# GpSimd in a state-space scan: the row product of a pair moves from the first place to the second

## The chip, the core and the metric

The kernel is written for one core of one Trainium2 chip, each engine's instructions by hand, with semaphores between them. A core has TensorE (PE, the matrix unit, with its weight loads as PEld), VectorE (DVE), ScalarE (ACT), GpSimd (POOL) and SyncE (SP, which issues DMAs here). An engine works through its own queue in order. The metric is the device time of a run in microseconds; the number to predict is the median of such runs.

## What is computed

Two layers follow each other over x of shape 4 x 1024 x 128: attention with a mixture of experts, and then a selective state-space layer (Mamba) with a second mixture of experts. The change lies in the recurrence of the state-space layer:

```python
dA = jnp.exp(dt_t[..., None] * A)
hstate = dA * hstate + (dt_t * u_t)[..., None] * B_t[:, None, :]
y_t = jnp.einsum('bdn,bn->bd', hstate, C_t)
...
y = jnp.swapaxes(ys, 0, 1) + u * D
y = y * jax.nn.silu(z)
```

There are 256 channels and 16 states to a channel; `A` depends on channel and state, `B_t` and `C_t` are one number for each state and time step, shared by all channels.

## The kernel before

`mamba_scan` keeps 128 channels on the 128 partitions, so the 256 channels make two halves (`half` 0 and 1), and time (1024 steps) runs along the free dimension. For each of 4 sequences it goes through the 16 states, two at a time: that is a pair `p`, 8 to a sequence (`JB`), 32 in all. Within a pair, `odd` 0 and 1 is the first and the second state. One tile of work is always 128 x 1024 numbers. For a pair the engines do this (written with (odd, half)):

- PE, **spread** (L1685, two matmuls in bf16): writes the row B of a state to all partitions of a PSUM tile, for (0,0), (0,1) and (1,0). There are two such PSUM tiles, one for each half (`inputs(half)`), so a spread waits until the last scan that read the tile is done.
- DVE, **input** (L1746): multiplies the spread row by `dtu`, which is dt * u (L1741, `times_u`, once for a sequence and half), in PSUM. Three of them in a pair.
- POOL, **row product** (L1808, `ms_x_row`): the same product for the fourth combination (1,1), from `b_row` in SBUF, a row of B brought in by a DMA.
- ACT: the decays exp(dt * A) (L1729 for three scans, L1732 for the fourth, into PSUM).
- DVE, **scan** (L1759): the recurrence, four in a pair, (0,0), (0,1), (1,0), (1,1), each into its own part of `h` (the tile `xnT` in the profile).
- POOL, **weigh** (L1801, `ms_ch`): the scanned state times the row C, four in a pair, into one of two tiles, one for each half. It waits for the scan of the same (odd, half), for the row of C, and for the add that read the tile before.
- PE, **add** (L1694, four matmuls in f32 against the identity, `x4` in the profile): adds the weighed state into the sums of its half in PSUM.
- In pairs 4 and 5 of a sequence PE adds u * D too (L1701, `skip`); at the first pair of the next sequence DVE reads the sums out (L1764, `gate`), between its scans.
- SP: loads `b_row` for a pair when the row product of the pair before is done (L1671), and after it the two rows of C (L1665) into a ring of four.

All loops are unrolled, and what stands in them sets the order of each queue. DVE, in a pair: input (0,0), input (0,1), scan (0,0), scan (0,1), input (1,0), scan (1,0), scan (1,1). At the end of a sequence `times_u` for the next stands behind scan (1,0) and behind scan (1,1). PE:

```python
for p in range(PAIRS_ALL):
    spread(p, 1, 0)
    add(p, 0, 0)
    if p + 1 < PAIRS_ALL:
        spread(p + 1, 0, 0)
    add(p, 0, 1)
    if p + 1 < PAIRS_ALL:
        spread(p + 1, 0, 1)
    add(p, 1, 0)
    ...
    add(p, 1, 1)
```

POOL, in a pair: row product, weigh (0,0), weigh (0,1), weigh (1,0), weigh (1,1). The row product waits for its row of B, for `dtu`, and for scan (1,1) of the pair before, which reads `x_row`; scan (1,1) of its own pair waits for it.

Of the kernel before, what the change touches and what calls it, by code (L numbers as in the profile page):

```python
# [1360 lines left out]
DI = 2  # L1361
# [256 lines left out]
def mamba_scan(nc, g, m):  # L1618


    with ExitStack() as ctx:
# [29 lines left out]
        def scans(p, odd, half):  # L1651

            return 4 * p + 2 * odd + half + 1
# [5 lines left out]
        @block.sync  # L1659
        def _(sp):  # L1660
            def c_row(p, odd):
                s = 2 * p + odd
                if p >= C_RING // 2:
                    sp.wait_ge(ch_ready, scans(p - C_RING // 2, odd, 1))
                sp.dma_start(c_rows[:, s % C_RING, :], g.bc_rows[NS + s % NS:NS + s % NS + 1, sequence(s // NS)].to_broadcast([P, T])).then_inc(c_in[s % C_RING], 16)  # L1665

            for p in range(PAIRS_ALL):
                n, b = 2 * p % NS + 1, p // JB
                if p > 0:
                    sp.wait_ge(x_row_ready, p)  # L1670
                sp.dma_start(b_row[:, :], g.bc_rows[n:n + 1, sequence(b)].to_broadcast([P, T])).then_inc(b_in, 16)  # L1671
                c_row(p, 0)
                c_row(p, 1)
# [115 lines left out]
        @block.gpsimd  # L1789
        def _(pool):  # L1790
            for half in range(DI):
                pool.tensor_tensor(diag[:, half, :], g.ident[:, :], m.d[:, half:half + 1].to_broadcast([P, P]), ALU.mult).then_inc(diag_ready, 1)

            def weigh(p, odd, half):
                s = 2 * p + odd
                if half == 0:
                    pool.wait_ge(c_in[s % C_RING], C_BASE + 16 * (s // C_RING + 1))
                pool.wait_ge(scanned, scans(p, odd, half))
                if s > 0:
                    pool.wait_ge(summed, scans((s - 1) // 2, (s - 1) % 2, half))  # L1800
                pool.tensor_tensor(ch[:, half, :], h[:, odd, half, :], c_rows[:, s % C_RING, :], ALU.mult).then_inc(ch_ready, 1)  # L1801

            for p in range(PAIRS_ALL):
                pool.wait_ge(b_in, 16 * (p + 1))
                pool.wait_ge(dtu_ready, DI * (p // JB) + 2)
                if p > 0:
                    pool.wait_ge(scanned, scans(p - 1, 1, 1))
                pool.tensor_tensor(x_row[:, :], dtu[:, 1, :], b_row[:, :], ALU.mult).then_inc(x_row_ready, 1)  # L1808
                for odd in range(2):
                    for half in range(DI):  # L1810
                        weigh(p, odd, half)


def mamba_out(nc, g, m):
# [352 lines left out]
```

## Time and profile before

| | us |
|---|---|
| three timed runs | 1480.87, 1481.11, 1486.27 |
| median | 1481.11 |
| the profiled execution: its own time | 1482.99 |
| its span, first to last instruction | 1481.1 |
| `mamba_scan` in it, from the first `times_u` to the last `gate` | 881.9 to 1307.4, 425.5 |

| engine | busy in the whole span, us | busy from 898 to 1300 us, of 402 us |
|---|---|---|
| PE | 1214.6 | 310.85 |
| DVE | 1153.7 | 391.20 |
| ACT | 672.6 | 132.41 |
| POOL | 653.5 | 364.15 |

In the profile a line names the source line, the engine, the operation, what is written and read, the shapes and how many instructions are merged. `[2.19 <-POOL ms_ch L1801]` behind it says that the engine was idle 2.19 us before and that POOL's product on L1801 ended this. The times are starts, counted from the start of the span, and durations. On DVE and POOL a duration overlaps the next instruction's start by 0.05 to 0.1 us, so a chain on one engine is measured from start to start; ends on PE are modelled. The granted clock (PEclk) is 1.00 at 2.4 GHz and 0.50 at 1.2 GHz.

### The profile page before, as it was taken

How to read it: one execution, taken by the hardware profiler on the slowest of the kernel's cores; microseconds unless marked ns; L12 is line 12 of the kernel's file. 1: busy time of each engine (PE TensorE's matmuls, PEld its weight loads, DVE VectorE, ACT ScalarE, POOL GpSimd, SP SyncE). 2: the span in 40 equal slices, each digit the busy share in tenths (PEclk: the TensorE clock that was granted, in tenths of full speed). 3: DMA queues.
4: the chain of work that ended last, by engine and by line, in shares of the span. 5: the costliest groups of instructions: out<-in, count | busy, mean ns of one | idle time of the engine just before them, and what ended most of it. 6: DMA issues, size and time to landing. Idle time of an engine off the chain costs nothing. (4 is left out here: it accounts for less than half of the span.)

```text
span 1481.1 us, 21354 instructions
## 1 busy us (share of the span) xinstructions
PE 1214.6 (82%) x7478; PEld 548.8 (37%) x7478; DVE 1153.7 (78%) x1366; ACT 672.6 (45%) x1057; POOL 653.5 (44%) x468
## 2 busy tenths in 40 slices
PE   4937999998999789879978767877877867766998
PEld 2412334333344344444444212322322322355565
DVE  5868999998996256747556889999999999964554
ACT  2515999997897413212215783333333323302221
POOL 2320000101002166636743068989989989921000
PEclk9956999999999889989997868999999999995999
DMA  4321111312101443313520013343333333400331
GB/s 105 121 94 44 57 50 51 115 48 77 50 25 46 103 112 112 110 57 105 120 50 18 6 51 128 128 128 104 117 119 128 128 100 115 126 9 24 68 57 43
DMA packets 75346, 120.37 MB, mean 81 GB/s; under 512 B 13246, under 2 KB 42758, under 8 KB 75254
## 3 DMA queue, kind: packets, MB, share of 16 engines
q1 hardware_dynamic: 75254, 119.16, 27.2%
q8 instruction: 56, 0.92, 0.3%
q14 instruction: 36, 0.29, 0.1%
HBM read 105.09 MB, written 13.63 MB: 80 GB/s over the span
## 5 line engine op out<-in xcount | busy, mean ns | idle before, releaser
L635 DVE TENSOR_REDUCE att_found<-PS 128x2 f32<-128x1024 f32 (+2 forms) x288 | 333.2, 1219 | 17.9 <-PE PS L738 16.1
L705 ACT ACTIVATE att_prob<-PS 128x512 f32<-128x512 f32 x576 | 313.6, 596 | 42.5 <-PE PS L760 30.5
L1694 PE MATMUL PS<-ms_ch,ident_sb 128*128 128x512 f32 x512 | 269.0, 651 | 72.6 <-POOL ms_ch L1801 72.6
L1801 POOL TENSOR_TENSOR ms_ch<-xnT,ms_c_rows 128x1024 f32<-128x1024 f32 x128 | 304.8, 2392 | 41.3 <-DVE xnT L1759 21.3
L1759 DVE TENSOR_TENSOR_SCAN xnT<-ms_decay,PS 128x1024 f32<-128x1024 f32 x96 | 216.1, 2276 | 4.2
L779 PE MATMUL PS<-att_prob,att_v 128*32 128x256 f32 (+1 forms) x2560 | 183.9, 374 | 2.8 <-ACT att_out L694 2.6
L1694 PEld LDWEIGHTS PS<-ms_ch,ident_sb 128*128 128x128 f32 x512 | 98.6, 204 | 194.8 <-POOL ms_ch L1801 107.5
L1732 ACT ACTIVATE PS<-m_dt,m_a 128x1024 f32<-128x1024 f32 x32 | 35.8, 1118 | 260.5 <-DVE xnT L1759 260.5
L738 PE MATMUL PS<-kr,qr 55*128 55x128 bf16 (+4 forms) x1152 | 121.4, 292 | 30.8 <-PEq L260 15.6
L760 PE MATMUL PS<-qr,kr 55*128 55x128 bf16 (+4 forms) x1152 | 115.3, 278 | 15.5 <-ACT att_prob L705 9.1
L1746 DVE TENSOR_TENSOR PS<-ms_dtu,PS 128x1024 f32<-128x1024 f32 x96 | 114.7, 1213 | 6.8 <-PE PS L1685 6.7
L1183 ACT ACTIVATE f_h<-PS,e_w_b 128x512 f32<-128x512 f32 x64 | 44.0, 687 | 159.3 <-PE PS L1311 159.3
L1729 ACT ACTIVATE ms_decay<-m_dt,m_a 128x1024 f32<-128x1024 f32 x96 | 106.2, 1138 | 13.3 <-DVE xnT L1759 13.3
L1162 POOL TENSOR_TENSOR f_yT<-f_yT,f_prod 128x512 f32<-128x512 f32 x56 | 70.9, 1267 | 93.6 <-DVE f_prod L1260 92.3
L1250 DVE SCALAR_TENSOR_TENSOR f_x3s<-PS,e_w_b,f_mask_row 128x512 f32<-128x512 f32 x64 | 47.9, 749 | 75.3 <-PE PS L1315 73.7
L1151 POOL TENSOR_TENSOR f_xm<-xnT,f_gate_row 128x512 f32<-128x512 f32 x64 | 81.0, 1267 | 40.1 <-DMA f_gate_row<-gate_rows_dram 37.9
L1685 PE MATMUL PS<-m_bc,m_w_sel_b 96*128 96x512 bf16 x192 | 64.0, 419 | 33.8 <-DVE xnT L1759 25.2
L738 PEld LDWEIGHTS PS<-kr,qr 48*128 48x128 bf16 (+1 forms) x1152 | 39.7, 97 | 137.7 <-issue 89.5
L779 PEld LDWEIGHTS PS<-att_prob,att_v 128*32 128x32 f32 x2560 | 55.1, 109 | 63.0 <-issue 53.7
L1808 POOL TENSOR_TENSOR ms_x_row<-ms_dtu,ms_b_row 128x1024 f32<-128x1024 f32 x32 | 75.2, 2348 | 1.7 <-DMA ms_b_row<-bc_rows_dram 1.7
L1320 PE MATMUL PS<-f_h,e_w_w 128*128 128x512 f32 x128 | 66.9, 605 | 10.8 <-DVE f_prod L1260 10.8
L1759 DVE TENSOR_TENSOR_SCAN xnT<-PS,ms_x_row 128x1024 f32<-128x1024 f32 x32 | 72.5, 2266 | 0.0
(222 smaller groups left out, 1632.5 us busy)
## 6 DMA issues: line engine op xcount, KB each, us to landing
ms_c_rows<-bc_rows_dram SPq DMA_DIRECT2D x64, 512.0 KB, 5.9
f_gate_row<-gate_rows_dram SPq DMA_DIRECT2D x64, 256.0 KB, 3.4
ms_b_row<-bc_rows_dram SPq DMA_DIRECT2D x32, 512.0 KB, 3.6
f_mask_row<-mask_rows_dram SPq DMA_DIRECT2D x64, 128.0 KB, 3.0
qk_parts_dram<-qkv_parts SPq DMA_DIRECT2D x48, 128.0 KB, 1.9
heads_dram<-att_out SPq DMA_DIRECT2D x16, 256.0 KB, 2.7
f_mask_row<-mask_rows_dram SPq DMA_DIRECT2D x64, 64.0 KB, 3.3
qr<-qk_parts_dram SPq DMA_DIRECT2D x32, 96.0 KB
```

Of the source, the lines that this page charges most:

```text
L635: dve.tensor_reduce(found[:, :, pair, first:first + (n - 1) * step + 1:step], PS[:, bank:bank + 2, :].rearrange("p r (w n) -> p r w n", w= ...
L705: act.activation(prob[:, step % PROB_RING * GH + h, :], PS[:, SCORE_BANK + unit % SCORE_RING, :], ACT.Exp, scale=float(D) ** -0.5).then_in ...
L738: last = pe.matmul(PS[:, MAX_BANK + 2 * (m % 2) + r, at:at + n], rows(qr, count, i, pair, r, q_block * P, P), rows(kr, count, i, pair, r, ...
L760: last[r] = pe.matmul(PS[:, SCORE_BANK + (unit + r) % SCORE_RING, col:col + w], rows(kr, count, i, pair, r, j * P, P), rows(qr, count, i, ...
L779: last = pe.matmul(PS[VW * h:VW * (h + 1), VALUE_BANK, q - half * CH:q - half * CH + w], v1[:, i % 2, half, h, j, :], prob[:, step % PROB_ ...
L1151: pool.tensor_tensor(xm[:, e % XM_RING, :], xnT[:, c * CH:(c + 1) * CH], gate_row[:, e % ROW_RING, :], ALU.mult).then_inc(xm_ready, 1)
L1694: last = pe.matmul(PS[:, Y_BANK + 2 * half + q, :], g.ident[:, :], ch[:, half, q * CH:(q + 1) * CH], start=j == 0 and not odd, stop=j == J ...
L1729: act.activation(decay[:, 2 * odd + half, :], m.dt[:, half, sequence(b)], ACT.Exp, scale=m.a[:, half, n + odd:n + odd + 1]).then_inc(decay ...
L1746: dve.tensor_tensor(inputs(half), dtu[:, half, :], inputs(half), ALU.mult).then_inc(input_ready, 1)
L1759: dve.tensor_tensor_scan(h[:, odd, half, :], factor, x, 0.0, ALU.mult, ALU.add).then_inc(scanned, 1)
L1801: pool.tensor_tensor(ch[:, half, :], h[:, odd, half, :], c_rows[:, s % C_RING, :], ALU.mult).then_inc(ch_ready, 1)
L1808: pool.tensor_tensor(x_row[:, :], dtu[:, 1, :], b_row[:, :], ALU.mult).then_inc(x_row_ready, 1)
```

## The change

In POOL's part of `mamba_scan` the first weigh of a pair is put ahead of the row product. Nothing else is touched: the same instructions with the same waits, 5 to a pair on POOL, in the order weigh (0,0), row product, weigh (0,1), weigh (1,0), weigh (1,1).

```diff
@@ -1801,14 +1801,15 @@
             for p in range(PAIRS_ALL):
+                weigh(p, 0, 0)
                 pool.wait_ge(b_in, 16 * (p + 1))
                 pool.wait_ge(dtu_ready, DI * (p // JB) + 2)
                 if p > 0:
                     pool.wait_ge(scanned, scans(p - 1, 1, 1))
                 pool.tensor_tensor(x_row[:, :], dtu[:, 1, :], b_row[:, :], ALU.mult).then_inc(x_row_ready, 1)
-                for odd in range(2):
-                    for half in range(DI):
-                        weigh(p, odd, half)
+                weigh(p, 0, 1)
+                weigh(p, 1, 0)
+                weigh(p, 1, 1)
```

POOL's queue for pairs 2 and 3, with the semaphores that each instruction waits for. `ms_ch` is a weigh, `ms_x_row` the row product, `ring_in0` to `ring_in3` the landing of a row of C (0 and 1 for the two states of an even pair, 2 and 3 for those of an odd one). Before:

```order
L1808 TENSOR_TENSOR ms_x_row<-ms_dtu,ms_b_row 128x1024 [waits ms_scanned,ms_dtu_ready,ms_b_in]
L1801 TENSOR_TENSOR ms_ch<-xnT,ms_c_rows 128x1024 [waits ms_summed,ms_scanned,ring_in0]
L1801 TENSOR_TENSOR ms_ch<-xnT,ms_c_rows 128x1024 [waits ms_summed,ms_scanned]
L1801 TENSOR_TENSOR ms_ch<-xnT,ms_c_rows 128x1024 [waits ms_summed,ms_scanned,ring_in1]
L1801 TENSOR_TENSOR ms_ch<-xnT,ms_c_rows 128x1024 [waits ms_summed,ms_scanned]
L1808 TENSOR_TENSOR ms_x_row<-ms_dtu,ms_b_row 128x1024 [waits ms_scanned,ms_dtu_ready,ms_b_in]
L1801 TENSOR_TENSOR ms_ch<-xnT,ms_c_rows 128x1024 [waits ms_summed,ms_scanned,ring_in2]
```

The same place of POOL's queue in the changed kernel (the row product's line is now L1809):

```order
L1801 TENSOR_TENSOR ms_ch<-xnT,ms_c_rows 128x1024 [waits ms_summed,ms_scanned,ring_in0]
L1809 TENSOR_TENSOR ms_x_row<-ms_dtu,ms_b_row 128x1024 [waits ms_scanned,ms_dtu_ready,ms_b_in]
L1801 TENSOR_TENSOR ms_ch<-xnT,ms_c_rows 128x1024 [waits ms_summed,ms_scanned]
L1801 TENSOR_TENSOR ms_ch<-xnT,ms_c_rows 128x1024 [waits ms_summed,ms_scanned,ring_in1]
L1801 TENSOR_TENSOR ms_ch<-xnT,ms_c_rows 128x1024 [waits ms_summed,ms_scanned]
L1801 TENSOR_TENSOR ms_ch<-xnT,ms_c_rows 128x1024 [waits ms_summed,ms_scanned,ring_in2]
```

The row product has changed places with weigh (0,0): the row product of a pair now stands behind an instruction that waits for a scan of that pair, and so does the load of the next rows, which SP issues behind it. Everything from weigh (0,1) on stands where it stood.

POOL's queue at the last pair, before:

```order
L1808 TENSOR_TENSOR ms_x_row<-ms_dtu,ms_b_row 128x1024 [waits ms_scanned,ms_dtu_ready,ms_b_in]
L1801 TENSOR_TENSOR ms_ch<-xnT,ms_c_rows 128x1024 [waits ms_summed,ms_scanned,ring_in2]
L1801 TENSOR_TENSOR ms_ch<-xnT,ms_c_rows 128x1024 [waits ms_summed,ms_scanned]
L1801 TENSOR_TENSOR ms_ch<-xnT,ms_c_rows 128x1024 [waits ms_summed,ms_scanned,ring_in3]
L1801 TENSOR_TENSOR ms_ch<-xnT,ms_c_rows 128x1024 [waits ms_summed,ms_scanned]
L1621 UNCONDITIONAL_BRANCH
```

and after:

```order
L1801 TENSOR_TENSOR ms_ch<-xnT,ms_c_rows 128x1024 [waits ms_summed,ms_scanned,ring_in2]
L1809 TENSOR_TENSOR ms_x_row<-ms_dtu,ms_b_row 128x1024 [waits ms_scanned,ms_dtu_ready,ms_b_in]
L1801 TENSOR_TENSOR ms_ch<-xnT,ms_c_rows 128x1024 [waits ms_summed,ms_scanned]
L1801 TENSOR_TENSOR ms_ch<-xnT,ms_c_rows 128x1024 [waits ms_summed,ms_scanned,ring_in3]
L1801 TENSOR_TENSOR ms_ch<-xnT,ms_c_rows 128x1024 [waits ms_summed,ms_scanned]
L1621 UNCONDITIONAL_BRANCH
```

Here too four weighs and one row product stand before the end of the stage, and the row product comes second.

## Rows read from the trace of the kernel before

**Rows 1.** Windows: stretch, us; busy PE, PEld, DVE, ACT, POOL; clock, DMA
```profile
898.00:1300.00 402.00, 310.85 (x712) 115.72 (x711) 391.20 (x229) 132.41 (x121) 364.15 (x156) 0.94 0.36 118
```

**Rows 2.** Waits of DVE from 885 to 1308 us: total, times, longest
```profile
DVE PS L1746 <- PE PS L1685: 6.7, 12, 1.3
DVE m_u L1764 <- PE PS L1694: 3.4, 2, 2.4
```

**Rows 3.** Timeline of one pair at the full clock: start, duration, what
```profile
1005.20 4.46 DVE L1759 TENSOR_TENSOR_SCAN xnT<-ms_decay,PS 128x1024 f32<-128x1024 f32 x2
1005.70 2.36 POOL L1808 TENSOR_TENSOR ms_x_row<-ms_dtu,ms_b_row 128x1024 f32<-128x1024 f32 x1
1005.80 1.99 PE L1694 MATMUL PS<-ms_ch,ident_sb 128*128 128x512 f32 x4 [0.38 <-POOL ms_ch L1801]
1007.62 0.60 PE L1685 MATMUL PS<-m_bc,m_w_sel_b 96*128 96x512 bf16 x2
1008.00 4.68 POOL L1801 TENSOR_TENSOR ms_ch<-xnT,ms_c_rows 128x1024 f32<-128x1024 f32 x2
...
1010.91 2.29 DVE L1759 TENSOR_TENSOR_SCAN xnT<-ms_decay,PS 128x1024 f32<-128x1024 f32 x1
1013.11 2.27 DVE L1759 TENSOR_TENSOR_SCAN xnT<-PS,ms_x_row 128x1024 f32<-128x1024 f32 x1
1013.25 0.61 PE L1685 MATMUL PS<-m_bc,m_w_sel_b 96*128 96x512 bf16 x2 [0.86 <-DVE xnT L1759]
1013.33 4.75 POOL L1801 TENSOR_TENSOR ms_ch<-xnT,ms_c_rows 128x1024 f32<-128x1024 f32 x2 [0.65 <-DVE xnT L1759]
...
1015.29 2.33 DVE L1746 TENSOR_TENSOR PS<-ms_dtu,PS 128x1024 f32<-128x1024 f32 x2
...
1017.54 2.28 DVE L1759 TENSOR_TENSOR_SCAN xnT<-ms_decay,PS 128x1024 f32<-128x1024 f32 x1
```

**Rows 4.** Timeline of the next pair, where the add runs slowly
```profile
1022.74 3.64 PE L1694 MATMUL PS<-ms_ch,ident_sb 128*128 128x512 f32 x4 [2.19 <-POOL ms_ch L1801]
...
1028.37 0.60 PE L1685 MATMUL PS<-m_bc,m_w_sel_b 96*128 96x512 bf16 x2
...
1029.07 1.23 DVE L1746 TENSOR_TENSOR PS<-ms_dtu,PS 128x1024 f32<-128x1024 f32 x1 [0.23 <-PE PS L1685]
```

**Rows 5.** Windows, columns as in Rows 1: the stretch of the slow add
```profile
1022.70:1026.10 3.40, 3.36 (x4) 1.28 (x5) 3.27 (x3) 3.08 (x4) 2.30 (x1) 0.50 0.98 325
```

**Rows 6.** The weigh's line: duration ns min/median/max, first and last start
```profile
L1801 POOL TENSOR_TENSOR ms_ch<-xnT,ms_c_rows x128: 2335/2356/3252, 889.5 to 1301.7; 128x1024 f32<-128x1024 f32 x128
```

**Rows 7.** Timeline at the end of the second sequence: times_u beside weighs
```profile
1089.10 1.20 DVE L1741 TENSOR_TENSOR ms_dtu<-m_dt,m_u 128x1024 f32<-128x1024 f32 x1
...
1089.31 6.51 POOL L1801 TENSOR_TENSOR ms_ch<-xnT,ms_c_rows 128x1024 f32<-128x1024 f32 x2 [0.66 <-DVE xnT L1759]
...
1092.41 1.20 DVE L1741 TENSOR_TENSOR ms_dtu<-m_dt,m_u 128x1024 f32<-128x1024 f32 x1
```

**Rows 8.** Timeline in the first mixture of experts: both engines read two SBUF tiles
```profile
586.60 1.26 POOL L1162 TENSOR_TENSOR f_yT<-f_yT,f_prod 128x512 f32<-128x512 f32 x1 [7.10 <-DVE f_prod L1260]
586.62 1.33 DVE L833 TENSOR_TENSOR fr_tmp<-fr_s,fr_w 128x64 f32<-128x64 f32 x1
```

**Rows 9.** The same line L833, duration ns min/median/max
```profile
L833 DVE TENSOR_TENSOR fr_tmp<-fr_s,fr_w x4: 224/776/1331, 478.9 to 675.5; 128x64 f32<-128x64 f32 x4
```

**Rows 10.** Timeline of the end of the scan stage
```profile
1299.43 4.64 POOL L1801 TENSOR_TENSOR ms_ch<-xnT,ms_c_rows 128x1024 f32<-128x1024 f32 x2 [0.68 <-DVE xnT L1759]
...
1304.13 1.98 PE L1694 MATMUL PS<-ms_ch,ident_sb 128*128 128x512 f32 x4 [0.32 <-POOL ms_ch L1801]
1306.15 1.22 DVE L1764 TENSOR_TENSOR m_u<-PS,m_sz 128x1024 f32<-128x1024 f32 x1 [1.08 <-PE PS L1694]
```

**Rows 11.** Timeline, DVE alone, the last pair
```profile
1291.30 4.46 DVE L1759 TENSOR_TENSOR_SCAN xnT<-ms_decay,PS 128x1024 f32<-128x1024 f32 x2
```

**Rows 12.** The line that loads the rows of C, L1665: issue to landing
```profile
DMA to landing us min/median/max: 4.5/5.9/7.7
```

## The prediction

> **What bounds the kernel now.** I read four views in this order. First the busy time by stretch: in 402 us of the scan stage DVE is busy 391, POOL 364, PE 311 [rows 1], so DVE is nearly full and POOL is not far behind. Second, DVE's waits: in the whole stage only 6.7 us, 12 times, on a spread from PE, and 3.4 us at the end on the last adds [rows 2]; nothing on POOL by name. Third, the timeline of one pair [rows 3]: scan (0,0) starts at 1005.20 and that of the next pair at 1017.54, so a pair costs 12.34 us, and DVE has no idle time in it. POOL needs five products of 2.34 us, 11.7 us, in the same time: 0.6 us of room. Last, the next pair [rows 4, 5]: PE had sat idle 2.19 us for a weigh, the granted clock fell to 0.50, the add took 3.64 us where it takes 1.98 at full clock [rows 3], and the next spread came 0.23 us late for DVE. Such cases are the 6.7 us. So the stage is DVE's as long as the results that DVE needs from PE come in time, and PE works behind POOL's weighs in a fixed order. The question is who is late once POOL's order changes.
>
> **The change part by part.** It adds and removes no instruction. It moves the row product behind weigh (0,0), and that one waits for scan (0,0) of its own pair. Times below are counted from the end of scan (0,0), 1005.20 + 2.28 = 1007.48 in rows 3.
>
> *The new ring.* Before, POOL does the row product while DVE is in scan (0,0), from 1005.70 to 1008.00, so that it costs nothing there [rows 3]. Now POOL has done with the pair before by 1005.70 and waits, until the scan ends and 0.13 us more for the semaphore (scan (1,0) ends at 1013.20, POOL starts at 1013.33 [rows 3]). Then come weigh (0,0), 2.33 us from start to start, the row product, 2.30, and weigh (0,1), 2.36 [rows 3], so weigh (0,1) ends at 7.1. Before it ended at 1012.68, which is 5.2. Who waits: add (0,1) on PE, and behind it in PE's queue spread (0,1) for the next pair, without which DVE can't do input (0,1) and then scan (0,0). That closes a ring from one scan (0,0) to the next: 0.13 + 6.99 + 0.05 until PE starts (a weigh ends 0.05 us after the next product's start at 1005.70, PE starts at 1005.80) + 1.82 for an add that waited (1005.80 to 1007.62) + 0.60 for the spread + 0.10 to DVE (1028.97 to 1029.07 [rows 4]) + 1.13 from input (0,1) to scan (0,0) (1016.41, which is the second of the two at 1015.29, to 1017.54) + 2.28 = 13.10 us. DVE alone needs 12.34. The difference, 0.76, is a new wait of DVE before input (0,1), once in each step from pair to pair. Of the 31 steps, six have 2.2 us more work on DVE (two times_u in the last pair of a sequence, two gates in the first of the next, at three places), which makes 14.6 there and hides the ring. 25 x 0.76 = **+19.0**.
>
> *The waits that were there.* The 12 waits of 6.7 us lie in ordinary pairs, at the same place, in front of input (0,1). They are at most 1.3 us each [rows 2] and fall inside the new wait or count in the next term. **-6.7**.
>
> *The clock.* Between 898 and 1300 us the mean granted clock is 0.94 [rows 1], so some 48 us of the 402 lie at the low level, 14 stretches like that in rows 5. They cost only 6.7 us so far, since PE had slack. Now an add and a spread lie on the ring, 2.3 us at full clock, and an add that runs at the low one costs 3.64 - 1.98 = 1.7 us more, all of it on DVE's path. Ends: 0, if the clock stays up because PE's longest idle time gets shorter (from 2.2 us to two of about 1.3 and 0.9, with the spread (0,0) in between), and 14 x 1.7 = 24, if each stretch meets that add. The idle time now lies just ahead of the very add that is on the ring, which speaks for the upper half; a low share of 12% spread evenly over 25 x 2.3 us would cost 7. I take six hits, **+10**.
>
> *The ends of sequences.* times_u is a DVE product of two SBUF tiles. At 1089.10 and 1092.41 it started 0.2 us ahead of POOL's weighs and took its 1.20 us; the two weighs took 6.51 us together and not 4.68 [rows 7]; the longest weigh is 3.25 us against 2.36 [rows 6]. The other way round, in the experts' stage, a DVE product of two SBUF tiles that began 0.02 us after POOL took 1.33 us, to POOL's end, and not 0.22 [rows 8, 9]. In the changed order POOL is in weigh (0,1) from 4.8 to 7.1 when times_u comes up at 5.7, so DVE stands until 7.1, some 1.4 us; the second one stands 0.2 us more. Three ends of sequences, where DVE is the bound: 3 x 1.6 = **+4.8**. Its ends: 0 if DVE isn't held, 3 x 2 x 2.3 = 14 if both stand a whole weigh.
> The Trainium skill says the same as these rows in "SBUF — State Buffer", section "Who interferes with whom": a DVE instruction with two SBUF inputs and a GpSimd instruction that reads SBUF exclude each other for a whole instruction, and who is first decides. It speaks against this change, and the rows agree with it. By a reader's plain assumption that engines don't touch each other, the sum would be 4.8 lower.
>
> *The tail.* The last scan (0,0) ends at 1291.30 + 2.28 = 1293.58 [rows 11], the last gate at 1307.37 [rows 10]: 13.8 us. Now five products stand in that stretch, 0.13 + 11.7, then an add of 1.98 + 0.07, then 0.11 and the gate of 1.22 [rows 10]: 15.2. **+1.4**.
>
> *What costs nothing.* Scan (1,1) needs the row product at 5.63 (1013.11); it is done at 0.13 + 2.33 + 2.35 = 4.8, so 0.8 us are left. SP's loads are issued behind the row product, 4.3 us later than before; the rows of C land 5.9 us after the issue, 7.7 at most [rows 12], so by 13.0 in the worst case, and are first used at 13.2. The row of B comes ahead of them in the same queue and is needed 2.3 us later. ACT's decays hang on scans alone. If the cover of the row product goes, each 0.1 us beyond 0.8 costs 2.5 us.
>
> **The sum.** 19.0 - 6.7 + 10 + 4.8 + 1.4 = +28.5. Against the profiled execution that is 1482.99 + 28.5 = 1511.5. That execution lies 1.9 us above the median of the runs, 1481.11; the same sum there gives **1509.6**.
>
> **The rivals.** (a) *The clock stays up.* The ring is as above, but PE's idle time is split and the clock no longer falls: +18.5, **1499.6**. For it speaks that the low adds follow an idle time of 2.2 us [rows 4], which no longer occurs; against it, that PE still does only one short spread between two adds there.
> (b) *The clock falls in front of the add again and again.* 14 hits or more: +42.5, **1523.6**. The Trainium skill, "TensorE: Matmul & The Clock Gate", section "HAM oscillation — how this bites in real kernels", tells of this pattern, a matrix unit that waits between bursts and starts each one at the low clock; the slow add in rows 4 agrees, and by that page the time would be this one.
> (c) *The row product is late.* If weigh (0,0) starts 1 us later than I think, since a row of C lands late, the ring grows by that 1 us (and scan (1,1) waits 0.2 us in it): 25 x 1 on top, **1534.6**. The landing times [rows 12] speak against it.
> (d) *Not slower.* Place: POOL's start on weigh (0,0). It is no longer behind the row product, so add (0,0) runs some 0.4 us earlier, and the slow adds no longer push spread (0,1) back; that gives back the 6.7 us and leaves the tail and the ends of sequences to pay, 1481.11 - 6.7 + 1.4 + 4.8 = **1480.6**, or 1475.8 if times_u then isn't held. It decides where the ring is no longer than DVE's 12.34, so where the three products take 6.2 us and not 7.0, 2.07 each. The shortest of 128 weighs took 2.335 [rows 6]. It would also hold if PE did spread (0,1) ahead of the add that stands before it; in rows 3 PE goes through its matmuls in the order of the code.
>
> **How the numbers follow.** Forecast 0.66, (a) 0.14, (b) 0.10, (c) 0.04, (d) 0.06, half of which is no measurable change. The forecast's own range, with four to nine hits on the clock and 0 to 8 us at the sequences' ends, is 1503 to 1518. To hold the time 8 times in 10, it is widened down to (a) and up halfway to (b): 1499 to 1520. Faster by over 0.5%, which is about the least that a measurement of this kernel can tell from no change, 0.03; within 0.5% 0.03; slower 0.94.
>
> **What would show it.** The changed profile should have scans (0,0) 13.1 us apart in most pairs, DVE's wait for spreads at about 25 to 30 us in 25 pieces or so with the longest over 2 us, POOL idle about 1.4 us ahead of weigh (0,0) only, its other four products back to back, times_u at 2.5 us or more three times, and no wait of scan (1,1). If the steps are 12.34 us apart, the ring is wrong. If they are 13.1 but the sum is 10 us off, it is the clock. If DVE waits in front of scan (1,1), it is the cover of the row product.

## The result

| | before | changed | ratio, 95% interval |
|---|---|---|---|
| timed runs, us | 1480.87, 1481.11, 1484.33, 1486.27 | 1519.25, 1521.03, 1523.22, 1523.42 | |
| median, us | 1482.72 | 1522.12 | 1.026 (1.0233 to 1.0288) |
| span of the profiled execution, us | 1481.1 | 1521.4 | |

The change costs 2.6%, 39 us. Slower was forecast, but by 28.5 us, with 1509.6 as the time and 1520 as the upper end of the range. The measured median lies 2 us outside it. The forecast was added to 1481.11, the median of three runs; with a fourth run the kernel before stands at 1482.72, so 1.6 us of the 12.5 between forecast and measurement are that base. The direction and most of the mechanism hold, and the size of one term was off; the experiments are about which one.

DVE's waits in the changed kernel, from 888 to 1348 us, answer to [rows 2]:

```profile
DVE PS L1746 <- PE PS L1685: 36.3, 33, 2.4
DVE m_u L1764 <- PE PS L1694: 6.2, 2, 4.6
```

The 6.7 us in 12 pieces have become 36.3 us in 33, where 25 to 30 us in some 25 pieces were forecast. DVE doesn't wait for the row product, and the releaser is PE's spread, as forecast. The next rows are of the timeline, one ordinary pair of the changed kernel and the next (start, duration, what; compare [rows 3]):

```profile
929.52 4.46 DVE L1759 TENSOR_TENSOR_SCAN xnT<-ms_decay,PS 128x1024 f32<-128x1024 f32 x2
...
931.93 2.34 POOL L1801 TENSOR_TENSOR ms_ch<-xnT,ms_c_rows 128x1024 f32<-128x1024 f32 x1 [1.51 <-DVE xnT L1759]
...
934.24 2.36 POOL L1809 TENSOR_TENSOR ms_x_row<-ms_dtu,ms_b_row 128x1024 f32<-128x1024 f32 x1
934.33 1.98 PE L1694 MATMUL PS<-ms_ch,ident_sb 128*128 128x512 f32 x4 [1.43 <-POOL ms_ch L1801]
...
936.55 4.65 POOL L1801 TENSOR_TENSOR ms_ch<-xnT,ms_c_rows 128x1024 f32<-128x1024 f32 x2
...
937.44 2.26 DVE L1759 TENSOR_TENSOR_SCAN xnT<-PS,ms_x_row 128x1024 f32<-128x1024 f32 x1
937.58 0.60 PE L1685 MATMUL PS<-m_bc,m_w_sel_b 96*128 96x512 bf16 x2 [1.26 <-DVE xnT L1759]
938.95 3.61 PE L1694 MATMUL PS<-ms_ch,ident_sb 128*128 128x512 f32 x4 [0.77 <-POOL ms_ch L1801]
...
942.40 0.60 PE L1685 MATMUL PS<-m_bc,m_w_sel_b 96*128 96x512 bf16 x2
...
943.10 1.23 DVE L1746 TENSOR_TENSOR PS<-ms_dtu,PS 128x1024 f32<-128x1024 f32 x1 [2.28 <-PE PS L1685]
944.24 2.28 DVE L1759 TENSOR_TENSOR_SCAN xnT<-ms_decay,PS 128x1024 f32<-128x1024 f32 x1
```

This is the ring, piece by piece. POOL waits 1.51 us for scan (0,0), then works without a gap; scan (1,1) starts at 937.44 and the row product had ended by 936.6, so its cover held. Add (0,1) starts at 938.95. Here it ran at the low clock, 3.61 us and not 1.98, and DVE waited 2.28 us in front of input (0,1). The step from 929.52 to 944.24 took 14.72 us. The step ahead of it, from scan (0,0) at 916.42 to 929.52, had the add at full clock and a wait of 0.66 us, and took 13.10, and at the end of the first sequence (994.64) the same idle pieces, 1.52, 1.27 and 0.77 us, stood ahead of an add at full clock:

```profile
916.42 4.46 DVE L1759 TENSOR_TENSOR_SCAN xnT<-ms_decay,PS 128x1024 f32<-128x1024 f32 x2
...
925.86 1.98 PE L1694 MATMUL PS<-ms_ch,ident_sb 128*128 128x512 f32 x4 [0.44 <-POOL ms_ch L1801]
...
928.38 1.23 DVE L1746 TENSOR_TENSOR PS<-ms_dtu,PS 128x1024 f32<-128x1024 f32 x1 [0.66 <-PE PS L1685]
...
994.64 1.98 PE L1694 MATMUL PS<-ms_ch,ident_sb 128*128 128x512 f32 x4 [0.77 <-POOL ms_ch L1801]
```

Of the 32 adds (0,1) of the changed kernel, 14 ran at the low clock, wholly or in part: nine in ordinary steps, three in the first pair of a sequence, one in the last pair of the second sequence, where it cost nothing (the step took 15.97 us as its neighbours did), and one in the tail. In the kernel before it was mostly add (0,0) that ran slowly, 15 times of 32, and slack behind it took up most of the delay before it reached DVE.

At the end of the first sequence (answers to [rows 7]) the first times_u comes 0.9 us after POOL has begun weigh (0,1), and takes 2.55 us:

```profile
992.23 8.97 POOL L1801 TENSOR_TENSOR ms_ch<-xnT,ms_c_rows 128x1024 f32<-128x1024 f32 x3
...
993.12 2.55 DVE L1741 TENSOR_TENSOR ms_dtu<-m_dt,m_u 128x1024 f32<-128x1024 f32 x1
```

In the first pair of the next sequence the spread (0,0) and the add (0,1) behind it run at the low clock, and the step takes 16.85 us where DVE alone needs 14.6:

```profile
1011.48 1.03 PE L1685 MATMUL PS<-m_bc,m_w_sel_b 96*128 96x512 bf16 x2 [2.68 <-DVE xnT L1759]
...
1012.30 3.62 PE L1694 MATMUL PS<-ms_ch,ident_sb 128*128 128x512 f32 x4
```

The tail, answering to [rows 10]. The slow add also keeps its tile from POOL, whose last weigh starts 1.55 us late:

```profile
1338.23 5.36 PE L1694 MATMUL PS<-ms_ch,ident_sb 128*128 128x512 f32 x8 [2.63 <-POOL ms_ch L1801]
...
1342.03 2.35 POOL L1801 TENSOR_TENSOR ms_ch<-xnT,ms_c_rows 128x1024 f32<-128x1024 f32 x1 [1.55 <-PE PS L1694]
...
1343.64 1.23 DVE L1764 TENSOR_TENSOR m_u<-PS,m_sz 128x1024 f32<-128x1024 f32 x1 [4.64 <-PE PS L1694]
```

With the starts of scan (0,0) of all 32 pairs, the scan stage splits like this in the profiled executions (us, "last" is the step out of the last pair of a sequence, "behind" the one after it):

| | before | changed | difference | forecast |
|---|---|---|---|---|
| 25 ordinary steps | 315.2 | 342.7 | +27.5 | +22.3 |
| of it the ring, 25 x (13.11 - 12.34) | | | +19.2 | +19.0 |
| of it the old waits | 6.7 | | -6.7 | -6.7 |
| of it nine slow steps of 14.7 to 14.85 | | | +15.0 | +10 (six) |
| 3 last steps | 43.8 | 47.9 | +4.1 | +4.8 |
| 3 steps behind | 45.2 | 49.7 | +4.5 | 0 |
| from the last scan (0,0) to the last gate | 16.1 | 18.9 | +2.8 | +1.4 |
| what stands ahead of the first scan | 887.1 | 888.5 | +1.4 | 0 |
| sum | | | +40.3 | +28.5 |

### The profile page after: what moved, and what is told of

Read it like the earlier page. It is cut to its first block and busy times, and to the rows that moved or that the text cites. A ratio compares the mean times of both kernels' runs of the same rounds, so it can differ in the third digit from the quotient of the medians.

```text
span 1521.4 us, 21354 instructions
## 1 busy us (share of the span) xinstructions
PE 1232.6 (81%) x7478; PEld 551.5 (36%) x7478; DVE 1159.8 (76%) x1366; ACT 672.6 (44%) x1057; POOL 653.8 (43%) x468
## 5 line engine op out<-in xcount | busy, mean ns | idle before, releaser
L635 DVE TENSOR_REDUCE att_found<-PS 128x2 f32<-128x1024 f32 (+2 forms) x288 | 333.3, 1218 | 18.0 <-PE PS L738 16.2
L1694 PE MATMUL PS<-ms_ch,ident_sb 128*128 128x512 f32 x512 | 279.7, 674 | 71.3 <-POOL ms_ch L1801 71.2
L1746 DVE TENSOR_TENSOR PS<-ms_dtu,PS 128x1024 f32<-128x1024 f32 x96 | 116.4, 1216 | 36.6 <-PE PS L1685 36.3
L1729 ACT ACTIVATE ms_decay<-m_dt,m_a 128x1024 f32<-128x1024 f32 x96 | 106.1, 1138 | 14.9 <-DVE xnT L1759 14.9
L1250 DVE SCALAR_TENSOR_TENSOR f_x3s<-PS,e_w_b,f_mask_row 128x512 f32<-128x512 f32 x64 | 47.9, 749 | 74.7 <-PE PS L1315 73.2
L1809 POOL TENSOR_TENSOR ms_x_row<-ms_dtu,ms_b_row 128x1024 f32<-128x1024 f32 x32 | 75.6, 2363 | 0.0
```

The costliest lines, as they stand in the source:

```text
L635: dve.tensor_reduce(found[:, :, pair, first:first + (n - 1) * step + 1:step], PS[:, bank:bank + 2, :].rearrange("p r (w n) -> p r w n", w= ...
L1694: last = pe.matmul(PS[:, Y_BANK + 2 * half + q, :], g.ident[:, :], ch[:, half, q * CH:(q + 1) * CH], start=j == 0 and not odd, stop=j == J ...
L1729: act.activation(decay[:, 2 * odd + half, :], m.dt[:, half, sequence(b)], ACT.Exp, scale=m.a[:, half, n + odd:n + odd + 1]).then_inc(decay ...
L1746: dve.tensor_tensor(inputs(half), dtu[:, half, :], inputs(half), ALU.mult).then_inc(input_ready, 1)
```

## The experiments

Each ran beside the kernel before on one chip. "Stage" is the time from the first scan to the last gate in the profiled execution, 420.3 us before and 459.2 us changed; it leaves out what precedes it, since the first scan began anywhere from 884.8 to 893.8 us in these runs. The profiled execution is one of a run's several and need not be its median. The cuts of code show what differs from the changed kernel, unless another one is named; "..." stands for lines left out.

**e1_after_fill: keep PE busy in its idle time.** The fillers are short matmuls with a tile of zeros, `zeros`, which POOL sets ahead of its work; they add zeros and leave the sums as they are (96x512 in the profile, not 128x512 as the text below has it).

```diff
+            def fill(n):
+                for k in range(n):
+                    pe.matmul(PS[:, Y_BANK + k % 2, :], zeros[:6 * NS, :], m.bc[:, 0:CH], start=False, stop=False)
...
                 spread(p, 1, 0)
+                if p % JB > 0:
+                    fill(3)
                 add(p, 0, 0)
+                fill(4)
                 if p + 1 < PAIRS_ALL:
                     spread(p + 1, 0, 0)
+                fill(3)
                 add(p, 0, 1)
```

> The changed kernel with short matmuls of zeros (bf16, 128x512, 0.22 us each, added to sums that they leave as they are) in PE's idle time of each pair: 3 ahead of add (0,0), 4 behind it, 3 ahead of add (0,1). Theory 'clock': the changed kernel's nine ordinary steps of 14.7 to 14.85 us and its long steps of 16.0 to 16.9 us behind the ends of sequences are adds at the low clock on the ring; with PE kept busy they go, ordinary steps are 13.1 us throughout, and the time is 13 to 20 us under the changed kernel's, so 1502 to 1509 us. Theory 'ring or port': the excess over the forecast is in POOL's or DVE's own work, the fillers change nothing or cost a little, 1520 to 1527 us.

Measured: 1500.53 us, ratio to the kernel before 1.0118 (1.0103 to 1.0133), so 1.4% under the changed kernel's 1.026. The stage took 438.8 us, 20.4 less: 14.0 in the ordinary steps, now all at 13.1 but the first of 13.8; 4.8 in the three steps behind the ends, and 1.6 in the tail. The windows view of 911 to 1307 us, first of the changed kernel and then of this one (columns as in [rows 1]):

```profile
911.00:1307.00 396.00, 294.25 (x638) 104.56 (x638) 357.80 (x206) 118.14 (x108) 325.87 (x139) 0.91 0.33 110
```

```profile
911.00:1307.00 396.00, 343.87 (x953) 129.71 (x953) 376.36 (x217) 127.58 (x117) 344.31 (x147) 0.99 0.35 116
```

The granted clock went from 0.91 to 0.99, and DVE got 18.6 us more work done in the same 396 us. The time is a shade under the expected range; the theory of the clock holds, its rival falls. The 20.4 us are a lower bound for what the clock costs, since fillers cost something themselves: the first step takes 13.81 us and not 13.13, where seven of them stand behind a slow add (0,0) and hold the next spread and add up. In the steps behind the ends, 14.96 us, three of them stand between the spread (0,0) and add (0,1), and add (0,1) starts only when they end. Without these e8 below has 14.60 at the full clock. So an estimate of the clock's whole cost is 20.4 + 0.7 + 3 x 0.36, some 22 us. The ring itself stands, since each step still has its 0.7 us:

```profile
1042.00 1.23 DVE L1757 TENSOR_TENSOR PS<-ms_dtu,PS 128x1024 f32<-128x1024 f32 x1 [0.66 <-PE PS L1687]
```

**e6 and e7: which idle time.** Of e1's fillers (the cuts are against e1), e6 keeps only those ahead of add (0,0), and e7 only those between add (0,0) and add (0,1).

```diff
-                fill(4)
-                fill(3)
```

```diff
-                if p % JB > 0:
-                    fill(3)
```

> The changed kernel with three matmuls of zeros ahead of add (0,0) alone, none between add (0,0) and add (0,1). Theory of the prediction's clock term, 'the clock falls for the idle time just ahead of the add on the ring': that idle time is as before, slow ordinary steps of 14.7 us stay, 7 to 10 of them, and the scan stage takes 453 to 460 us. Rival 'what PE does over the whole step decides': with 0.65 us more work in each step the slow steps go as they went in e1_after_fill, 438 to 443 us.

> The changed kernel with the matmuls of zeros between add (0,0) and add (0,1) alone, four and three. Theory 'idle time just ahead of the ring's add': the slow ordinary steps go altogether, all are 13.1 us, and the scan stage takes 438 to 443 us as with all fillers. Rival 'whole step': slow steps remain, some of them moved, 445 us or more.

Measured, in one run each: e6 1521.33 us, stage 454.5, seven ordinary steps of 14.7 to 14.8, and 12 of the 32 adds (0,1) slow. e7 1501.85 us, stage 439.1, no slow step but the first, 14.3. DVE's waits of e6 and then of e7:

```profile
DVE PS L1755 <- PE PS L1687: 33.0, 32, 2.4
```

```profile
DVE PS L1755 <- PE PS L1687: 19.0, 36, 1.6
```

Three short matmuls behind the ring's add took 4.7 us off the stage and left seven slow ordinary steps where there had been nine; seven ahead of it took off 20.1, nearly all that ten did. Both came as the theory of the place expected. But e7 also fills more than e6 (1.5 us a step against 0.65), and no run puts the same number in either place, so it isn't shown whether the place or the amount decides.

**e4_short_add: is PE's add on the ring?** Half of add (0,1) is left out in 28 of the 32 pairs, about a ninth of PE's sums (the text below says a quarter, which is too much).

```diff
+                short = half == 1 and not odd and j > 0
-                for q in range(CPB):
+                for q in range(1 if short else CPB):
```

> The changed kernel, where add (0,1) does only the first of its two halves in all pairs but the first of a sequence, so a quarter of PE's sums is left out. Theory 'ring through PE': the add on the ring is 0.86 us shorter, the ring is 13.1 - 0.86 = 12.25, below DVE's own 12.34, so ordinary steps are 12.34 to 12.4 us, slow adds cost 0.8 and not 1.7, and the time falls by some 25 us to 1493 to 1501 us. Rival 'DVE waits for POOL itself': scan (0,1) of the next pair waits for weigh (0,1), PE has no part in it, and the steps stay at 13.1, 1518 to 1523 us.

Measured: 1504.81 us, ratio 1.0147 (1.0127 to 1.0168). Seven ordinary steps, where the clock was high, took 12.34 us, DVE's own time, so the ring runs through the add. In such a pair the two inputs stand side by side without a wait:

```profile
927.15 2.33 DVE L1747 TENSOR_TENSOR PS<-ms_dtu,PS 128x1024 f32<-128x1024 f32 x2
...
928.81 1.98 PE L1695 MATMUL PS<-ms_ch,ident_sb 128*128 128x512 f32 x4 [0.76 <-POOL ms_ch L1802]
```

The size was missed, 1493 to 1501 expected. The clock fell more often, perhaps because PE had less to do, which no run takes apart: 0.87 from 898 to 1300 us, where the changed kernel has 0.92 and the kernel before 0.94 [rows 1], and steps of 13.0 to 13.6 us took part of the gain back, one even 16.2.

**e3_row_third: one place later.**

```diff
                 weigh(p, 0, 0)
+                weigh(p, 0, 1)
                 ...
                 pool.tensor_tensor(x_row[:, :], dtu[:, 1, :], b_row[:, :], ALU.mult).then_inc(x_row_ready, 1)
-                weigh(p, 0, 1)
```

> The changed kernel with the row product one place later still, behind weigh (0,1). Weigh (0,1) then is early, and scan (1,1) waits for the row product. Theory 'ring': the row product ends 7.1 us after scan (0,0), scan (1,1) wants it at 5.6, the ring goes through scan (1,1), both inputs and scan (0,0), and ordinary steps are 13.95 us: 0.13 + 6.99 + 0.1 + 2.2 + 1.13 + 1.13 + 2.28. DVE's waits are for ms_x_row and no longer for spreads; the time is 1528 to 1538 us. Rival 'what is moved late costs in proportion': the second place costs 0.76 us a step, the third twice that, the waits stay at the spreads, and steps are 13.9 by the spread. The named releaser of DVE's idle time tells them apart.

Measured in one run: 1521.63 us, stage 461.2, most ordinary steps 13.92 to 13.95. The releaser has changed:

```profile
DVE xnT L1759 <- POOL ms_x_row L1810: 39.3, 29, 1.8
DVE m_u L1764 <- PE PS L1694: 3.3, 2, 2.0
DVE PS L1746 <- PE PS L1685: 2.4, 3, 1.0
```

The step and the releaser came as worked out, and the rival falls. The time was missed, 1528 to 1538 us expected: this ring is longer by 0.8 us a step than the changed kernel's, yet the stage is longer by 2.0 us only and the time, in one run, the same. Its ring doesn't go through an add, so slow adds cost it little: a step with an add (0,0) of 3.59 us took 13.93, and two steps took 14.48 and 14.28. The clock was also higher, 0.95 from 898 to 1300 us. What the changed kernel loses to the clock, this one loses to the longer ring.

**e5: the old order at the ends of sequences alone**, with the fillers of e1 (against e1):

```diff
+                if p % JB < JB - 1:
+                    weigh(p, 0, 0)
                 ...
                 pool.tensor_tensor(x_row[:, :], dtu[:, 1, :], b_row[:, :], ALU.mult).then_inc(x_row_ready, 1)
+                if p % JB == JB - 1:
+                    weigh(p, 0, 0)
```

> The changed kernel with the matmuls of zeros of e1_after_fill, and in the last pair of each sequence the row product back in the first place. Theory 'times_u is held by a weigh under way': then times_u starts ahead of weigh (1,0) again, takes 1.20 us and not 2.55, and the three last steps of a sequence are 14.6 us and not 15.98, 4 us less in all than e1_after_fill; the steps behind them stay within 1.5 us of what they are there. Rival 'it is the ring that reaches over the ends': times_u takes its 2.55 us or the steps stay at 15.9 though it doesn't, and the scan stage takes what it took in e1_after_fill, 438.8 us.

Measured: 1505.35 us, ratio 1.0147 (1.0132 to 1.0162), stage 440.4. The last steps came down to 14.61 us as the theory says, and times_u to 1.20. The line of times_u in the changed kernel and in this one (ns, min/median/max):

```profile
L1741 DVE TENSOR_TENSOR ms_dtu<-m_dt,m_u x8: 1194/1440/2551, 883.3 to 1226.5; 128x1024 f32<-128x1024 f32 x8
```

```profile
L1752 DVE TENSOR_TENSOR ms_dtu<-m_dt,m_u x8: 1198/1200/1419, 884.2 to 1215.7; 128x1024 f32<-128x1024 f32 x8
```

But the steps behind them grew from 15.0 to 16.65 to 17.96 us, each with matmuls at the low clock in it, 6.4 us in all, which is more than the gain of 4.1. The second half of the expectation failed.

**e9 and e10: the ends again, with the clock held there too.** Both have twelve fillers behind add (0,0) in the first pair of a sequence, e9 with e5's order at the ends, e10 with the changed kernel's (against e1).

```diff
-                fill(4)
+                fill(4 if p % JB else 12)
```

> e5_fill_ends_old with twelve matmuls of zeros behind add (0,0) in the first pair of a sequence, where its PE sat idle and the clock fell three times, with steps of 16.65 to 17.96 us behind the ends. Theory 'the gain of the old order at the ends was given back to the clock': the last steps of a sequence stay at 14.61 us, those behind them come down to 14.6 to 15.0, and the scan stage takes 431 to 435 us. Rival 'the steps behind the ends are long for another reason, the weighs that times_u held up': they stay at 16.6 or more, 438 us or more.

> The same fillers with the changed kernel's order at the ends too, to be set beside e9_fill_all_ends_old. Theory 'times_u held by a weigh costs 1.37 us at each end': last steps 15.98, steps behind them 14.6 to 15.0, the scan stage 437 to 439 us, some 4 us more than e9_fill_all_ends_old. Rival: no difference between the two, since what waits longer at the end waits less behind it.

Measured: e9 1500.55 us, 1.0098 (1.0073 to 1.0123), stage 437.7; e10 1505.68 us, 1.0140 (1.0115 to 1.0164), stage 441.4. Last steps 14.61 against 15.99. Both stages missed their ranges, e9's by 2.7 us and e10's by 2.4, about as much as the first pair lost, where twelve fillers behind a slow add hold PE up (15.5 us for a step of 13.1). The steps behind the ends came down in e9, but to neither the 14.6 to 15.0 of the theory nor the 16.6 of its rival. Behind the ends e9 has 15.6 three times, each with the clock low, and e10 14.96 twice with the clock high and 15.62 where it fell. Like with like, at the third end, both low: 14.61 + 15.62 against 15.99 + 15.62, a difference of 1.4 us for an end. The stages differ by 3.6 us where some 4 were expected, and the intervals of the two ratios overlap only from 1.0115 to 1.0123; the rival of e10, no difference, falls. DVE in e9 and then in e10:

```profile
996.00 1.20 DVE L1752 TENSOR_TENSOR ms_dtu<-m_dt,m_u 128x1024 f32<-128x1024 f32 x1
997.12 2.28 DVE L1770 TENSOR_TENSOR_SCAN xnT<-PS,ms_x_row 128x1024 f32<-128x1024 f32 x1
```

```profile
991.73 2.57 DVE L1752 TENSOR_TENSOR ms_dtu<-m_dt,m_u 128x1024 f32<-128x1024 f32 x1
994.22 2.28 DVE L1770 TENSOR_TENSOR_SCAN xnT<-PS,ms_x_row 128x1024 f32<-128x1024 f32 x1
```

**e2 and e8: such fillers for the kernel before** (the cut is against it). e2 puts six ahead of add (0,0) in all pairs but the first of a sequence, e8 twelve more behind add (0,0) in the first (the last two lines).

```diff
                 spread(p, 1, 0)
+                if p % JB > 0:
+                    fill(6)
                 add(p, 0, 0)
+                if p % JB == 0:
+                    fill(12)
```

> The kernel before with six such matmuls of zeros ahead of add (0,0) of each pair but the first of a sequence, where PE sits idle for 2.2 us. Theory 'clock': the clock no longer falls ahead of that add, DVE's waits of 6.7 us for spreads shrink to 1 or 2, and the kernel is 4 to 6 us faster than the one before, about 1477 us. Rival: the fillers themselves delay the add or the spread, or the clock falls elsewhere; within 2 us of the kernel before.

> The kernel before with the matmuls of zeros of e2_before_fill, and twelve of them behind add (0,0) in the first pair of a sequence, where PE sat idle 3.5 us and the clock fell three times in e2_before_fill, each time with a late spread of 1.2 to 2.2 us. Theory 'clock': DVE no longer waits for a spread anywhere in the stage but in its first pairs, all ordinary steps 12.34 and those at the ends 14.6, the scan stage 413 to 415 us and the ratio to the kernel before 0.994 to 0.998. Rival: the fillers hold up the spread behind them or the fall moves on; 417 us or more, ratio 0.998 to 1.001.

Measured: e2 1481.8 us, 0.9993 (0.9981 to 1.0006), stage 417.3; e8 1480.3 us, 0.998 (0.9968 to 0.9992), stage 415.6. In e2 the ordinary steps were all 12.34 but the first, and the steps behind the ends took 15.9, 15.9 and 16.9 us. In e8 those came down to 14.6 and 15.0, and the first step went up from 12.7 to 14.9 us. e2 fell short of its expectation: its rival came, the clock fell elsewhere. e8 landed inside its own by the ratio and 0.6 us beyond it by the stage. DVE's waits of e8:

```profile
DVE PS L1757 <- PE PS L1687: 4.4, 5, 1.5
```

e8's median is the lowest of all, 2.9 us or 0.2% under the kernel before, with an interval that leaves out 1 by little. In the profiled execution the low clock costs that kernel 8.1 us, 6.7 in ordinary steps and 1.4 in one step behind an end.

## Why the prediction was half right

*The ring.* Right to two hundredths: 13.10 us forecast, 13.10 to 13.12 measured, +19.2 for +19.0. e4 shows that PE's add is part of it, e1 that it stays when the clock is high, and e3 that the reckoning works for another place of the row product too.

*The old waits.* Right in size, with a misreading that matters below. Eleven of the 12 waits lie in ordinary steps. The longest, 1.3 us, lies in the step behind the third end, which took 15.97 us before, where its two like took 14.60: there PE had a spread and an add at the low clock.

*The clock.* This is the step that failed. The mechanism was right, slow adds (0,1) on DVE's path, but the term was too small and left places out. The forecast took six slow adds at 1.7 us in ordinary steps, +10. There were nine, +15.0. For the steps behind the ends it took nothing, since DVE's extra 2.2 us were to hide the ring, and for the tail it took an add at full clock. At full clock DVE's extra work does about that: 14.96 us in e1, of which the fillers make some 0.36 by the estimate above. At the low clock it does not: the three steps took 49.7 us, 4.5 more than before and 5.9 more than 3 x 14.6, and the tail 1.6 more than in e1. By its own sign, steps of 13.1 and a sum 10 us off, the prediction pointed to the clock, and e1 confirms it: keeping PE busy takes 20.4 us off the stage, twice the forecast term. Six was also a choice against its own argument, which spoke for the upper half of 0 to 24. The upper end itself was near: 14 adds (0,1) ran slowly, as many as it had counted stretches at the low clock before, and the estimate from e1 is some 22 us. That the two counts are equal may be chance.

Rival (a) fell: PE's idle pieces in ordinary steps did get shorter, and the clock fell all the same. Rival (b), 1523.6, lies 1.5 us off the measured time, and with fourteen slow adds its mechanism and its count came; its sum is off in that not all lie on the ordinary ring at 1.7 us each. It had a chance of 0.10.

The Trainium skill, "TensorE: Matmul & The Clock Gate", section "HAM oscillation — how this bites in real kernels", tells of bursts that start at the low clock after each wait. The trace agrees in part: the add at 938.95 took 3.61 us for one of 1.98, but 18 of the 32 adds (0,1) ran at full clock, the one at 994.64 behind the same idle pieces.

*The ends of sequences.* Right in mechanism and nearly in size, 3 x 1.36 for 3 x 1.6, as e5, e9 and e10 confirm. The first times_u is held for 1.35 us; the second wasn't held at all (1.19 us), since it came up just as POOL changed instructions.

*The tail.* 1.4 forecast, 2.8 measured; 1.2 with the clock held (e1: 17.3 against 16.1), so the rest is the clock again, in the slow add at 1338.23, which also holds up POOL's last weigh.

*What costs nothing.* Right: DVE has no wait for the row product or for ACT, and POOL none that the profile puts down to a row of C.

*Ahead of the stage.* 1.4 us lie in code that wasn't changed. In e3 and e4, where that code is the same too, the first scan began at 886.1 and 890.9 us, so this is within the scatter of executions.

*The range.* Its upper end allowed for nine slow adds, and nine came in ordinary steps; it had nothing for the clock behind the ends and in the tail. (Its lower end, by its own terms four hits and nothing at the ends, comes out at 1501.6 and not 1503.)

## What to carry to other kernels

When an engine with room to spare is put in a ring with the bound one, look at what lies between: here weigh (0,1) ends 1.9 us later, and 0.76 of it reaches DVE in each step, through a matmul that DVE waited for in few steps before. And a matmul that comes onto the critical ring brings its clock with it: count the places where it can be slow, the ends of loops and the tail too, and take as the upper end that each low stretch of the kernel before meets it. Here that gave 24 us, against some 22 measured. Matmuls of zeros in PE's idle time are a cheap test for what the low clock costs; their own cost has to be looked for in the steps where they stand behind a slow matmul. As a remedy they gave 1.4% in the changed kernel and 0.2% in the one before.

## What the runs showed of the hardware

A DVE product of two SBUF tiles that comes up during a GpSimd product stands until that is done, 2.55 us and not 1.20, and the GpSimd product behind it is then held in its turn (three weighs 8.97 us, where three products back to back take 7.0). The direction in which DVE waits had one example before, of 1.33 us for 0.22 [rows 8, 9], and holds for a product that alone takes 1.20 us.

The granted clock fell to 1.2 GHz though PE's idle pieces ahead of the slow add at 938.95 were 1.43, 1.26 and 0.77 us, with an add and a spread in between: not one was as long as the 2.19 us ahead of the slow add before [rows 4]. The same pieces also stood ahead of adds at full clock (994.64), so they alone don't tell which add will be slow. Splitting idle time did not keep the clock up; filling it did (0.91 and 0.99 over the same 396 us).
